# A graph network's sums over neighbours, on TensorE: plain f32 products against f32r products with the rows split in two

## What is computed

```
A = (adj != 0).astype(x.dtype)
h = x
for l in range(weight.shape[0]):
    m = jnp.einsum('bnd,de->bne', h, weight[l])
    agg = jnp.einsum('bij,bid->bjd', A, m)
    h = _gru_cell(agg, h, w_ih, w_hh, b_ih, b_hh)
return h * mask[..., None]
```

## Time and profile before

| | |
|---|---|
| median of 3 runs | 550.27 us (550.24 to 550.37) |
| the profiled execution's own time | 550.48 us |
| its span, first to last instruction | 548.3 us |
| TensorE matmul busy | 522.3 us, 95% |
| VectorE busy | 438.4 us, 80% |
| ScalarE busy | 369.7 us, 67% |
| GpSimd busy | 251.9 us, 46% |
| the 80 windows of the network | from 40.0 us to about 540 us |

### The profile page before, as it was taken

The page is one execution under the profiler, slowest core; times in us unless marked ns, Lnnn a source line. Parts: engine busy times, 40 slices in busy tenths (PEclk is TensorE's granted clock), DMA queues, the critical chain, the costliest instruction groups (busy, mean ns, idle before and its releaser), DMA issues.

```text
span 548.3 us, 8516 instructions
## 1 busy us (share of the span) xinstructions
PE 522.3 (95%) x2991; PEld 445.8 (81%) x2991; DVE 438.4 (80%) x968; ACT 369.7 (67%) x683; POOL 251.9 (46%) x298
## 2 busy tenths in 40 slices
PE   7998999999999999999999999999999999999980
PEld 6886889877888888878888889888888888888860
DVE  5486565698988986889988986879988998878785
ACT  2446565667786676777785766787786678877644
POOL 7558232258452245457543245355553235433235
PEclk9799799999999999999999999999999999999995
DMA  6876610000000010000000000000000000100002
GB/s 150 204 183 159 160 34 2 1 0 1 2 1 1 0 33 20 21 20 21 0 2 1 0 1 21 20 20 20 0 2 0 2 1 19 36 24 0 1 0 77
DMA packets 35562, 17.28 MB, mean 32 GB/s; under 512 B 4305, under 2 KB 35482, under 8 KB 35522
## 3 DMA queue, kind: packets, MB, share of 16 engines
q1 hardware_dynamic: 32489, 15.12, 10.6%
q10 hardware_dynamic: 2393, 1.41, 0.9%
q0 software_dynamic: 640, 0.22, 0.3%
HBM read 12.54 MB, written 4.19 MB: 31 GB/s over the span
## 4 chain that ended last, share of the span: by engine, by line
PE 77%; DVE 10%; ACT 5%; POOL 4%; issue 2%; ACTq 1%; DMA 1%; DVEq 0%; POOLq 0%
PE p L1145 17%; PE p L1147 17%; PE p L1146 16%; PE p L1139 11%; PE p L1132 7%; PE p L1026 3%; PE p L1000 2%; DVE cg L943 2%; DVE cg L946 2%; PE p L1019 1%; DVE hT L850 1%; DVE dg L848 1%; PE p L1009 1%; POOL rs L420 1%; DMA rows<-in_L_gnn_b_hh_dram 1%
## 5 line engine op out<-in xcount | busy, mean ns | idle before, releaser
L457 POOL TENSOR_TENSOR dg<-hT,ng 128x512 f32<-128x512 f32 x80 | 124.8, 1560 | 267.4 <-ACT ng L661 267.4
L1145 PE MATMUL p<-hhi,wh 128*128 128x512 f32 x240 | 101.8, 424 | 0.9 <-DVE hlo L836 0.6
L1145 PE MATMUL p<-ghi,wf 128*128 128x512 f32 x240 | 101.1, 421 | 0.4 <-DVE glo L842 0.4
L1147 PE MATMUL p<-hhi,wh 128*128 128x512 f32 x240 | 94.8, 395 | 0.0
L1147 PE MATMUL p<-ghi,wf 128*128 128x512 f32 x240 | 94.4, 393 | 0.0
L1146 PE MATMUL p<-hlo,wh 128*128 128x512 f32 x240 | 94.1, 392 | 0.0
L1146 PE MATMUL p<-glo,wf 128*128 128x512 f32 x240 | 93.6, 390 | 0.0
L943 DVE SCALAR_TENSOR_TENSOR cg<-p,biasc,rg 128x512 f32<-128x512 f32 x80 | 59.9, 748 | 38.1 <-ACT rg L644 37.2
L644 ACT ACTIVATE rg<-p,gb 128x512 f32<-128x512 f32 x80 | 55.4, 692 | 35.5 <-PE p L1147 29.8
L661 ACT ACTIVATE ng<-cg,biasc 128x512 f32<-128x512 f32 x80 | 57.9, 723 | 24.9 <-DVE cg L946 24.7
L1139 PEld LDWEIGHTS p<-an,nat 128*128 128x128 f32 x512 | 66.9, 191 | 5.2
(11 more groups left out here) (138 smaller groups left out, 854.0 us busy)
## 6 DMA issues: line engine op xcount, KB each, us to landing
xn<-in_x_dram SPq DMA_DIRECT2D x8, 512.0 KB, 4.8
an<-in_adj_dram SPq DMA_DIRECT2D x8, 512.0 KB, 6.9
out_dram<-xn SPq DMA_DIRECT2D x16, 256.0 KB, 2.3
xt<-in_x_dram SPq DMA_DIRECT2D x16, 50.0 KB
w<-in_L_gnn_W_dram ACTq DMA_DIRECT2D x1, 640.0 KB, 6.3
w<-in_L_gnn_W_dram SPq DMA_DIRECT2D x1, 640.0 KB, 5.6
zg<-in_L_gnn_weight_dram ACTq DMA_DIRECT2D x1, 320.0 KB, 4.3
xt<-in_x_dram SPq DMA_DIRECT2D x8, 36.0 KB
```

What stands on the lines that cost most here:

```text
L457: nc.gpsimd.tensor_tensor(dg[:, w.k % 2, :], hT[:, w.slot, :], ng[:, w.k % 2, :], ALU.subtract).then_inc(d_ok, 1)
L1145: MM(bank[:], w[:, 0, cols], xhi, start=start, stop=False)
L1147: return MM(bank[:], w[:, 1, cols], xhi, start=False, stop=stop)
```

## The change

The stepped sums become f32r products. ScalarE's copy from PT is now written to `nhi` (f32r, the high half), VectorE gets a new operation `lo_rows` that writes `nlo` = PT - `nhi` (f32r), and TensorE makes two f32r products of 128 columns for each graph, `nhi` and `nlo` by the 0/1 adjacency, which add up in the same bank. The 0/1 adjacency goes to a buffer of its own, `ar` (f32r). `an` holds two chunks in place of four, and `ar` two as well; with that come two waits on SP ahead of the loads of chunks 2 and 3, and one on GpSimd ahead of `ones` from visit 8 on. The sums of entering visits stay f32 (`ar` read as f32).

```diff
-        an = sb("an", [128, B, N])
+        an = sb("an", [128, 2 * CB, N])
+        ar = sb("ar", [128, 2 * CB, N], f32r)
...
-        nat = sb("nat", [128, SLOTS, SB, D])
+        nhi = sb("nhi", [128, 2, SB, D], f32r)
+        nlo = sb("nlo", [128, 2, SB, D], f32r)
...
                 if c >= 2:
                     sp.wait_ge(xa_in, 64 * (c - 1))
+                    sp.wait_ge(a_ok, SLOTS * (c - 1) - 2)
+                    sp.wait_ge(a0_ok, 2)
                 load_chunk(sp, c)
...
-                ab = an[:, visit * SB:(visit + 1) * SB, :]
-                nc.gpsimd.tensor_scalar(ab, ab, 0.0, 0.0, ALU.is_equal, ALU.is_equal).then_inc(a_ok, 1)
+                b = visit * SB % (2 * CB)
+                if visit >= 2 * SLOTS:
+                    pool.wait_ge(G_ps, PER * (visit // SLOTS - 1))
+                nc.gpsimd.tensor_scalar(ar[:, b:b + SB, :], an[:, b:b + SB, :], 0.0, 0.0, ALU.is_equal, ALU.is_equal).then_inc(a_ok, 1)
...
-                    nc.scalar.copy(nat[:, w.old], PT[:].rearrange("p (b d) -> p b d", b=SB)).then_inc(nat_ok, 1)
+                    nc.scalar.copy(nhi[:, p], PT[:].rearrange("p (b d) -> p b d", b=SB)).then_inc(nat_ok, 1)
...
+            def lo_rows(w):
+
+                dve.wait_ge(nat_ok, w.turned + 1)
+                TT(nlo[:, w.k % 2], PT[:].rearrange("p (b d) -> p b d", b=SB), nhi[:, w.k % 2], ALU.subtract).then_inc(nlo_ok, 1)
...
                 if k and ALL_WINDOWS[k - 1].turn == "step":
                     lo_state(k + 2)
+                if w.out == "step":
+                    lo_rows(w)
...
-                        pe.wait_ge(nat_ok, w.turned + 1)
-                        aggregate(k + 2, PG, lambda q: nat[:, w.old, q, :])
+                        pe.wait_ge(nlo_ok, w.turned + 1)
+                        b = visit_of(k + 2) * SB % (2 * CB)
+                        for q in range(SB):
+                            to, ones_q = PG[:, q * N:(q + 1) * N], ar[:, b + q, :]
+                            MM(to, nhi[:, k % 2, q, :], ones_q, start=True, stop=False)
+                            last = MM(to, nlo[:, k % 2, q, :], ones_q, start=False, stop=True)
+                        last.then_inc(G_ps, 1)
```

More of the change, by code:

```diff
@@ L232, in build @@
             "na_ok", "nb_ok", "ya_ok", "yb_ok", "ha_ok", "hb0_ok", "hb1_ok", "sa_ok", "sb_ok", "oa_ok", "ob_ok", "x_ok", "a_ok"))
+        nlo_ok = sem("nlo_ok")
         r_ps, i_ps, z_ps, T_ps, X_ps, F_ps, G_ps = map(sem, ("r_ps", "i_ps", "z_ps", "T_ps", "X_ps", "F_ps", "G_ps"))
@@ L259, in load_half @@
         def load_half(eng, dst, src, b, done):
-            eng.dma_start(dst[:, b:b + CB // 2, :], src[b:b + CB // 2, :, :].rearrange("b n d -> n b d")).then_inc(done, 16)
+            at = b if dst is xn else b % (2 * CB)
+            eng.dma_start(dst[:, at:at + CB // 2, :], src[b:b + CB // 2, :, :].rearrange("b n d -> n b d")).then_inc(done, 16)
         def load_chunk(eng, c):
@@ L790, in ones @@
                 dve.wait_ge(a0_in[visit // 2], 16)
-                ab = an[:, visit * SB:(visit + 1) * SB, :]
-                TS(ab, ab, 0.0, 0.0, ALU.is_equal, ALU.is_equal).then_inc(a0_ok, 1)
+                b = visit * SB % (2 * CB)
+                TS(ar[:, b:b + SB, :], an[:, b:b + SB, :], 0.0, 0.0, ALU.is_equal, ALU.is_equal).then_inc(a0_ok, 1)
             def add(c, first, some=range(PACK)):
@@ L1135, in aggregate @@
             def aggregate(m, bank, src):
-                b = visit_of(m) * SB
+                b = visit_of(m) * SB % (2 * CB)
                 for q in range(SB):
-                    last = MM(bank[:, q * N:(q + 1) * N], src(q), an[:, b + q, :], start=True, stop=True)
+                    last = MM(bank[:, q * N:(q + 1) * N], src(q), ar[:, b + q, :].bitcast(f32), start=True, stop=True)
                 last.then_inc(G_ps, 1)
```

## The result

The changed kernel takes 568.87 us (567.92 to 570.54, 4 runs) against 550.25 us for the kernel before. The ratio is 1.036, with an interval of 1.034 to 1.039: 18.6 us slower. The forecast was 616 us. The direction came out as forecast, but the likeliest case did not happen; the first rival, equal price, had given 565.9.

The account below looks back on a forecast made before the run. The prediction took TensorE's stream as the bound. The profiled 550.5 us plus 59.2 for the products plus 6.6 for VectorE gave 616.3, with the runs' median 0.2 lower: 616 us, range 561 to 622.

Parts of the forecast that it names:

- the likeliest case: Stepped sums on TensorE: a narrow f32r product is dear, 0.223 to 0.2305 us; 616 us in all, chance 0.52.
- the first rival: Stepped sums: a new matmul costs 0.111 us, as an old record did; only VectorE's operation adds time; 566 us, chance 0.36.
- the price of a narrow f32r product: TensorE's stepped sums: 0.227 us for each of 512 new matmuls against 0.111 for each old record, adding 59.2 us.
- the natural floor: TensorE's stepped sums: 0.111 us a new matmul, set by loading 128 stationary columns, equal to what goes.
- VectorE's part: 64 new operations of 690 ns, hidden in windows without plan work, making TensorE's sums wait in others: net +6.6 us.
- ScalarE's copy: ScalarE's copy of the rows to f32r: 569 ns in place of 592, no effect on the time.
- waits for `nlo`: TensorE's sums waiting for VectorE's new operation: about 3.0 us in each middle stage, 0.7 in the first, 0.9 in the last.
- late `hT`: Equal-price case, windows 10 to 16 of the first three stages: full VectorE delays `hT`, about 2.6 us a stage, 7.8 in all.
- The forecast of what TensorE would wait for: Ahead of sums, `nlo` for 0.5 to 1.2 us in middle stages' windows 2, 3, 6, 8; at equal price, transposes for `hT`.
- x: Price of one new f32r matmul of 128 columns in TensorE's stepped sums; 0.227 us taken, path change 512 (x - 0.111) us.
- SP, GpSimd and buffers: Chunk 2's small rows on SP start at about 150 us, with 30 us of cover; GpSimd's new wait too costs nothing.
- The third rival: `lo_rows` on VectorE costs more than 690 ns; 0.1 us more on each of 64 adds 3.5 us; no chance of its own.

Follow-up runs that it names:

- e2: Changed kernel without `lo_rows`, `nhi` multiplied twice, sums waiting for ScalarE's rows: 550.9 us, ratio 1.0035 to the kernel before.
- e6: e2 with each product moving 256 columns, the adjacency of two graphs, in place of 128: 550.8 us, a single run.
- e3: e2 with `lo_rows` running, TensorE waiting for it only before the next transposes into the same bank: 560.7 us, ratio 1.022 to the kernel before.
- e1: Changed kernel's buffers and queue waits alone, with f32 rows and sums and no `lo_rows`: 547.9 us, ratio 1.000 to the kernel before.
- e11: e2 with rows and 0/1 adjacency in bf16, eight products a sum, a second 0/1 copy written: 540.6 us, a single run.
- e8: Changed kernel with the high half only, four f32r products a sum, no `lo_rows`: 533.3 us, ratio 0.972 to the kernel before.
- e5: e2 with each product moving 64 columns of the adjacency in place of 128: 548.6 us, a single run.
- e7: e2 with 64 of 128 feature columns of the rows loaded as stationary operand: 535.6 us, a single run.

## Why the prediction was wrong

**The step that failed** is the price of a narrow f32r product. The prediction bounded it rightly, 0.058 to 0.23 us by the wide f32r product, named the load of 128 stationary columns as what holds narrow f32 records at 0.109, called 0.111 "the natural floor", and then took a value near the upper end, 0.227, because the only f32r products in the trace were 0.23 us. That term was 59.2 us and measured 1.3 us by the windows of e2. It treated the price of a 512-column product as a price of the data type, though 512 columns at one cycle each are 0.213 us of it. The rows for the other value were all there: narrow products at 0.109 whatever their moving width (rows 5), and a recorded load of 191 ns for both types (rows 4). The 17 ns by which a wide f32r product exceeds its columns was the only row against, and it was given too much weight. e6 shows 0.119 us on average where 256 columns are 0.107: that fits an extra that counts where streaming limits and is hidden where the load does, but one width doesn't show it, and what the extra consists of wasn't tried.

**VectorE's part** held in mechanism and roughly in size. Forecast for window 22 was a wait of 1.2 us: measured 1.16 idle, and the window grew by 1.4 (1.36 in window 42, its like in the next stage). Windows 23, 26 and 28: forecast 0.8, 0.6 and 0.5, measured growth 0.9, 0.7 and 0.6. Windows without plan work: forecast nothing, measured within 0.05. The operation cost 687 ns, forecast 690. ScalarE's copy stayed at 592 ns, where 569 was forecast, which changed nothing.

The rival's sum had 7.6 us of waits for `nlo` and 7.8 us of late `hT`, 15.4 in all. The trace has 19.7 in windows 3 to 78, of which e2 gives 1.3 to the products, so some 18 are VectorE's. The side that came out too small is the second: e3 leaves 12 us without the sums' wait, against 7.8, and so leaves 6 to 7 for that wait. By windows e3 has 8.5 us in windows 9 to 17, close to the 7.8, and 2.7 in windows 2 to 8, of which the forecast had nothing. The forecast of what TensorE would wait for did not come true either: with the sums waiting for `nlo`, its matmuls stand idle ahead of the transposes for 6.6 us as before, and the loss of windows 9 to 17 stands ahead of the sums. That the rival's 565.9 us came within 3 us of 568.87 is in part luck, since 2.0 us of clock in windows 1 and 2, for which nobody had reckoned, pulled the traced time its way. (With x at 0.125 the rival's own sum gives 573 and not the 571 that stands there.)

**SP, GpSimd and buffers**: forecast nothing, e1 ratio 1.000.

**The clock** was no term of the forecast. From window 3 until some 14 us before the end it stood at its upper level in both traces, and the end is as long in both, so none of the loss there is a matter of the clock. In windows 1 and 2 it was at the lower level for 6.8 us in the kernel before alone, as shown above. Single executions are the quicker the higher their mean granted clock: the changed kernel took 567.92 us at a mean granted clock of 0.982 and 570.54 at 0.977, and the kernel before, beside e1, 546.45 at 0.984 and 551.04 at 0.976.

**The third rival**, a dearer `lo_rows` because GpSimd and VectorE get in each other's way, didn't happen: 687 ns on average over 64.

## What to carry to other kernels

Ask of a matmul first how many stationary columns it loads, then how many columns it moves. With 128 stationary f32 or f32r columns and 64 to 256 moving ones the load was the price here, and neither a data type that streams faster nor fewer moving columns helped; a quicker load (e11) or fewer loads (e8) did. Splitting an operand into two halves makes two products with a load each: eight f32r loads cost what the eight records of four f32 matmuls cost, so it won nothing. And an engine at 80% on average can be full in just those windows where the plan has put other work: read its idle time ahead of the new operation's place window by window, and put the operation ahead of what nobody waits for.

## What the runs showed of the hardware that was not expected

- An f32r product of 128 stationary columns costs 0.11 us with 64 moving columns (e5), 0.114 with 128 (e2), 0.119 with 256 (e6) and 0.23 with 512 (rows 2). There is no penalty for a narrow one.
- The load of a bf16 operand of 128 columns is recorded at 98 ns (e11), that of f32 and f32r at 191 (rows 4, e2), of 64 f32r columns at 135 (e7, the row below); products follow each other at 0.06, 0.11 and 0.06 us.

```profile
L1268 PEld LDWEIGHTS p<-ar,nhi 128*64 128x64 f32 x256 | 32.6, 135 | 2.6
```

- 6.8 us at the lower clock level cost some 2.0 us of the kernel's time. One execution had them and another hadn't, after the same 2.3 us of idle time on TensorE.
